# Splitting the layer-1 query weights ahead of the expert blocks, with six buffers for finished expert rows

## The reference, cut to what matters

```python
w, idx = jax.lax.top_k(p, TOPK)                       # 2 of 16 experts for each of 1024 tokens
gu = jnp.einsum('th,ehf->etf', x, gate_up_proj)
gate, up = jnp.split(gu, 2, axis=-1)
inter = jax.nn.silu(gate) * up
y = jnp.einsum('eti,eih->eth', inter, down_proj)
out = jnp.einsum('eth,te->th', y, combine)
...
q = (hidden_states @ Wq).reshape(N, t, H, DQ)         # layer 1; Wq is 256 x 2048
k = (hidden_states @ Wk).reshape(N, t, G, DQ)
v = (hidden_states @ Wv).reshape(N, t, G, DV)
```

## Time and profile before

| | us |
|---|---|
| median of 3 runs | 567.59 |
| lowest and highest | 564.04, 568.15 |
| profiled execution, its own time | 566.75 |
| span of that execution | 564.9 |

### The profile page before, as it was taken

The page is one execution under the profiler, slowest core; times in us unless marked ns, Lnnn a source line. Parts: engine busy times, 40 slices in busy tenths (PEclk is TensorE's granted clock), DMA queues, the critical chain, the costliest instruction groups (busy, mean ns, idle before and its releaser), DMA issues.

```text
span 564.9 us, 10664 instructions
## 1 busy us (share of the span) xinstructions
PE 508.0 (90%) x3547; PEld 438.8 (78%) x3570; DVE 394.8 (70%) x840; ACT 337.0 (60%) x755; POOL 308.7 (55%) x300
## 2 busy tenths in 40 slices
PE   8889999999996995699993798999999999999982
PEld 7568888888874884486772587999999899999882
DVE  2678888888872165749753688778866995578464
ACT  5546677777765244253340587768766866686552
POOL 4846777677763024639753168766544644466210
PEclk9999999999998997789996899999999999999996
DMA  8939999900000921243575000000000000000011
GB/s 279 391 113 372 305 323 316 313 13 0 0 0 1 368 116 56 82 128 106 160 253 209 23 0 2 1 1 1 2 2 0 1 1 2 2 1 2 1 38 39
DMA packets 17582, 56.80 MB, mean 101 GB/s; under 512 B 2580, under 2 KB 12314, under 8 KB 15738
## 3 DMA queue, kind: packets, MB, share of 16 engines
q1 hardware_dynamic: 14784, 49.81, 26.0%
q0 software_dynamic: 2752, 6.40, 3.2%
HBM read 49.19 MB, written 28.45 MB: 137 GB/s over the span
## 4 chain that ended last, share of the span: by engine, by line
PE 68%; DVE 10%; ACT 6%; issue 5%; DMA 5%; POOL 4%; SPq 1%; ACTq 0%; DVEq 0%; POOLq 0%
PE bank L435 10%; PE bank L437 8%; PE bank L436 8%; PE bank L483 5%; PE bank L525 4%; PE bank L544 3%; PE bank L906 3%; PE bank L527 2%; PE bank L668 2%; PE bank L653 2%; PE bank L655 2%; PE bank L654 2%; PE bank L555 2%; DMA wqk_raw<-in_wqk 2%; PE bank L923 2%
## 5 line engine op out<-in xcount | busy, mean ns | idle before, releaser
L999 ACT ACTIVATE probs<-bank,neg_max,q_scale 128x256 f32<-128x256 f32 (+1 forms) x128 | 63.7, 507 | 39.4 <-DVE neg_max L1565 39.4
L1775 POOL TENSOR_TENSOR probs<-probs,inv_sum 128x512 f32<-128x512 f32 x64 | 51.6, 827 | 44.0 <-DVE inv_sum L1573 44.0
L1808 POOL TENSOR_TENSOR exps<-exps,tables 128x256 f32<-128x256 f32 x32 | 25.2, 787 | 77.0 <-ACT exps L1092 77.0
L1795 POOL TENSOR_TENSOR swapped<-swapped,tables 128x512 f32<-128x512 f32 x32 | 42.9, 1339 | 24.0 <-ACT swapped L1030 23.8
L1092 ACT ACTIVATE exps<-bank 128x768 f32<-128x768 f32 x32 | 25.9, 810 | 42.2 <-PE bank L635 42.2
L1405 DVE TENSOR_TENSOR q_lo<-q_sum,q_hi 128x512 fp32r<-128x512 f32 x32 | 28.0, 877 | 28.4 <-ACT q_hi L1063 28.3
L1551 DVE TENSOR_TENSOR swapped<-bank,tables 32x512 f32<-32x512 f32 x64 | 44.4, 693 | 1.4
L1767 POOL TENSOR_TENSOR qT<-qT,swapped 128x512 f32<-128x512 f32 x32 | 40.8, 1274 | 7.1 <-DVE swapped L1551 7.1
L1911 POOL DMA_INDIRECT y_rows<-y_slot,dest x31 | 30.1, 972 | 23.7 <-DVE y_slot L1743 13.8
L435 PE MATMUL bank<-x,wq_hi 128*128 128x256 f32 x128 | 39.1, 306 | 2.7 <-DVE q_sum L1392 2.6
L525 PE MATMUL bank<-keysT,qT 128*128 128x256 f32 x128 | 38.3, 381 | 0.7 <-ACT wo_full L1214 0.7
(11 more groups left out here) (264 smaller groups left out, 1801.3 us busy)
## 6 DMA issues: line engine op xcount, KB each, us to landing
slots<-in_c_unused SPq DMA_DIRECT2D x20, 1036.0 KB, 36.9
gu_all<-in_gate_up SPq DMA_DIRECT2D x4, 1024.0 KB, 8.1
xg<-slots SPq DMA_DIRECT2D x31, 129.5 KB, 2.2
wvo_raw<-in_wvo SPq DMA_DIRECT2D x1, 2560.0 KB, 21.1
dn_all<-in_down SPq DMA_DIRECT2D x1, 2048.0 KB, 8.4
wq_full<-in_Wq SPq DMA_DIRECT2D x1, 2048.0 KB, 15.7
wo_raw<-in_Wo SPq DMA_DIRECT2D x1, 2048.0 KB, 10.7
yg<-y_rows SPq DMA_DIRECT2D x4, 512.0 KB, 5.2
```

Of the source, the lines that this page charges most:

```text
L999: ins = act.activation(probs[:, par, h, c0:c1], bank[:, 2 * par + h, c0:c1], ACT.Exp, bias=neg_max[:, par, i:i + 1], scale=q_scale[:, b, t ...
L1775: ins = pool.tensor_tensor(some, some, inv, ALU.mult)
L1795: pool.tensor_tensor(sw, sw, sin_rows(), ALU.mult).then_inc(at1["sin_done"], 1)
```

## The change

It has four parts.

1. **ACT**: the eight `wq_hi` copies stand in a row ahead of the first block's copy, behind the key and value copies, and none stands inside the blocks.
2. **POOL and DVE**: the key and value subtractions and the first four `wq_lo` chunks move from POOL to DVE, between the block table and `weights()`. POOL keeps the other four chunks, ahead of its first scatter of finished rows. None stands inside the blocks. A new semaphore `wq_lo` counts DVE's chunks.
3. **`y_slot`** has six buffers for four, so `copy_y(k)` waits for the landing of block k-6. KINDS (regions of filler rows, so that scatters in flight never write one address) grows from 6 to 8. `gated` and `act_tok` now lie in `swapped`, which is unused in this stage.
4. **SP** reads the block's address into a register before it waits for a free `xg` buffer, and no longer after.

```diff
-KINDS = 6
+KINDS = 8
+YS = 6
-        gated = sb("gated", [P, 2, FF], F32, blocks)
-        act_tok = sb("act_tok", [P, 2, FF], F32, blocks)
-        y_slot = sb("y_slot", [P, 4, D], F32, blocks)
+        y_slot = sb("y_slot", [P, YS, D], F32, blocks)
+    gated, act_tok = (swapped[:, i, 0:2 * FF].rearrange("p (i n) -> p i n", i=2) for i in range(2))
...
+        act.wait_ge(ld["wq1_in"], 16)
+        act.wait_ge(ln["y_done"], NT)
+        for i in range(PAIRS):
+            act.activation(chunk(wq_hi, i), chunk(wq_full, i), ACT.Copy).then_inc(kv["w_hi"], 1)
         copy_block(0)
         for k in range(STEPS):
             if k + 1 < STEPS:
                 copy_block(k + 1)
             silu(k)
-            if 2 <= k < 2 + PAIRS:
-                act.activation(chunk(wq_hi, k - 2), chunk(wq_full, k - 2), ACT.Copy).then_inc(kv["w_hi"], 1)
...
+        dve.wait_ge(kv["kv_hi"], 1)
+        dve.tensor_tensor(wk_lo[:], wk_raw, raw(wk_hi[:]), ALU.subtract).then_inc(kv["kv_lo"], 1)
+        dve.wait_ge(kv["kv_hi"], 2)
+        dve.tensor_tensor(wv_lo[:], wv_raw, raw(wv_hi[:]), ALU.subtract).then_inc(kv["kv_lo"], 1)
+        for i in range(PAIRS // 2):
+            dve.wait_ge(kv["w_hi"], i + 1)
+            dve.tensor_tensor(chunk(wq_lo, i), chunk(wq_full, i), raw(chunk(wq_hi, i)),
+                              ALU.subtract).then_inc(kv["wq_lo"], 1)
         weights()
...
-            if k >= 4:
-                dve.wait_ge(y_out[k % 4], 16 * (k // 4))
+            if k >= YS:
+                dve.wait_ge(y_out[k % YS], 16 * (k // YS))
...
-        pool.wait_ge(kv["kv_hi"], 1)
-        pool.tensor_tensor(wk_lo[:], wk_raw, raw(wk_hi[:]), ALU.subtract).then_inc(kv["kv_lo"], 1)
-        pool.wait_ge(kv["kv_hi"], 2)
-        pool.tensor_tensor(wv_lo[:], wv_raw, raw(wv_hi[:]), ALU.subtract).then_inc(kv["kv_lo"], 1)
+        for i in range(PAIRS // 2, PAIRS):
+            pool.wait_ge(kv["w_hi"], i + 1)
+            pool.tensor_tensor(chunk(wq_lo, i), chunk(wq_full, i), raw(chunk(wq_hi, i)),
+                               ALU.subtract).then_inc(kv["w_lo"], 1)
         for k in range(STEPS):
             pool.wait_ge(mo["dest_ready"], k + 1)
             pool.wait_ge(mo["y_copied"], k + 1)
             pool.indirect_dma_start(y_rows, ...)
-            if 3 <= k < 3 + PAIRS:
-                pool.wait_ge(kv["w_hi"], k - 2)
-                pool.tensor_tensor(chunk(wq_lo, k - 3), chunk(wq_full, k - 3), raw(chunk(wq_hi, k - 3)),
-                                   ALU.subtract).then_inc(kv["w_lo"], 1)
...
         for k in range(STEPS):
+            at_blocks = [sp.value_load(block_at[0:1, m:m + 1], ...) for m in ...]
             if k >= XG:
                 sp.wait_ge(mo["xgT_done"], k - XG + 1)
                 sp.wait_ge(mo["dest_ready"], k - XG + 1)
```

More of the change, by code:

```diff
@@ L288, in build @@
     xg_in = [sem(f"xg_in{j}") for j in range(XG)]
-    y_out = [sem(f"y_out{j}") for j in range(4)]
+    y_out = [sem(f"y_out{j}") for j in range(YS)]
     y_back = [sem(f"y_back{b}") for b in range(B)]
@@ L304, in build @@
               "xgT_done xgT_copied up_done silu_done act_ready actT_done actT_copied down_done y_copied dest_ready")
-    kv = sems("kv1", "kv_hi kv_lo w_hi w_lo k_done swap_done cos_done sin_done k_summed "
+    kv = sems("kv1", "kv_hi kv_lo w_hi wq_lo w_lo k_done swap_done cos_done sin_done k_summed "
               "k_hi k_lo v_done v_copied ones")
@@ L612, in pe_queries1 @@
             eng.wait_ge(kv["w_hi"], PAIRS)
-            eng.wait_ge(kv["w_lo"], PAIRS)
+            eng.wait_ge(kv["wq_lo"], PAIRS // 2)
+            eng.wait_ge(kv["w_lo"], PAIRS // 2)
         if m >= 2:
@@ L676, in pe_out1 @@
         if b == 0:
-            eng.wait_ge(kv["w_lo"], PAIRS + p + 1)
+            eng.wait_ge(kv["w_lo"], PAIRS // 2 + p + 1)
         elif p == 0:
@@ L1246, in _ @@
             silu(k)
-            if k == 2:
-                act.wait_ge(ld["wq1_in"], 16)
-                act.wait_ge(ln["y_done"], NT)
-            if 2 <= k < 2 + PAIRS:
-                act.activation(chunk(wq_hi, k - 2), chunk(wq_full, k - 2), ACT.Copy).then_inc(kv["w_hi"], 1)
         load_table(act, 2 * B + 8, ACT.Sqrt)
@@ L1740, in copy_y @@
             dve.wait_ge(mo["down_done"], k + 1)
-            if k >= 4:
-                dve.wait_ge(y_out[k % 4], 16 * (k // 4))
-            dve.tensor_copy(y_slot[:, k % 4, :], bank[:, down_bank(k), 0:D]).then_inc(mo["y_copied"], 1)
+            if k >= YS:
+                dve.wait_ge(y_out[k % YS], 16 * (k // YS))
+            dve.tensor_copy(y_slot[:, k % YS, :], bank[:, down_bank(k), 0:D]).then_inc(mo["y_copied"], 1)
         def find_rows(k):
@@ L1911, in _ @@
             pool.indirect_dma_start(y_rows, bass.IndirectOffsetOnAxis(ap=dest[:, k:k + 1], axis=0),
-                                    y_slot[:, k % 4, :], None).then_inc(y_out[k % 4], 16)
-            if 3 <= k < 3 + PAIRS:
-                pool.wait_ge(kv["w_hi"], k - 2)
-                pool.tensor_tensor(chunk(wq_lo, k - 3), chunk(wq_full, k - 3), raw(chunk(wq_hi, k - 3)),
-                                   ALU.subtract).then_inc(kv["w_lo"], 1)
+                                    y_slot[:, k % YS, :], None).then_inc(y_out[k % YS], 16)
         pool.memset(v_tok[:].rearrange("p b j g n -> p (b j g) n")[:, :, DV:DV + 1], 1.0).then_inc(kv["ones"], 1)
@@ L1943, in _ @@
         for i in range(REGIONS):
-            sp.dma_start(slots[i * REGION:(i + 1) * REGION, :], a["c_unused"][i % 4 if i < E else 4 + i % 2]).then_inc(ld["unused_in"], 16)
+            sp.dma_start(slots[i * REGION:(i + 1) * REGION, :], a["c_unused"][i % 6 if i < E else 6 + i % 2]).then_inc(ld["unused_in"], 16)
         sp.dma_start(wk_raw, a["Wk1"]).then_inc(ld["wkv1_in"], 16)
@@ L1954, in _ @@
         for k in range(STEPS):
+            at_blocks = [sp.value_load(block_at[0:1, m:m + 1], min_val=0, max_val=UNITS + NB - 1)
+                         for m in range(PER_STEP * k, PER_STEP * k + PER_STEP)]
             if k >= XG:
@@ L1957, in _ @@
                 sp.wait_ge(mo["dest_ready"], k - XG + 1)
-            for i in range(PER_STEP):
-                m = PER_STEP * k + i
-                at_block = sp.value_load(block_at[0:1, m:m + 1], min_val=0, max_val=UNITS + NB - 1)
+            for i, at_block in enumerate(at_blocks):
                 sp.dma_start(xg[ROWS * i:ROWS * i + ROWS, k % XG, :],
@@ L1963, in _ @@
         sp.dma_start(wo1_raw[:], a["Wo1"].rearrange("(h p) n -> p h n", p=P)).then_inc(ld["wo1_in"], 16)
-        for j in range(4):
-            sp.wait_ge(y_out[j], 16 * len(range(j, STEPS, 4)))
+        for j in range(YS):
+            sp.wait_ge(y_out[j], 16 * len(range(j, STEPS, YS)))
         for b in range(B):
```

## The result

| | before | after |
|---|---|---|
| median, us (4 runs each, same chip) | 567.38 | 560.98 |
| lowest and highest | 564.04, 568.15 | 559.11, 561.86 |
| profiled execution, its own time | 566.75 | 561.69 |
| its span | 564.9 | 559.9 |

The ratio of the times is 0.9882 with a 95% interval from 0.9835 to 0.9929: faster by 1.2%. The interval excludes no change, but it has a gain of 1% inside, so "over 1%" is likely and not certain; the change run again (e4) has 0.9892 (0.9854 to 0.993). The forecast of 562.3 lay 1.3 us above the median, and the range holds it. The median thus fell on the side to which the prediction gave the smaller chance (0.36 for over 1%, 0.61 for within 1%).

A forecast was written before the change was run, and what follows sets the result against it. The prediction took PE as the bound, held up in seven block rounds by POOL's subtraction holding DVE's `find_rows`. It summed 5.0 + 0.7 - 0.4 = 5.3 us, for a median of 562.3 us, range 560.3 to 566.0.

The forecast's parts named there:

- The loop: Expert blocks: the seven rounds with subtractions go at PE's 1.64 us each, 5.0 us less, bounds 4.8 to 5.3.
- It is therefore the subtraction that holds DVE's instruction: Blocks from 257 to 273.5 us: POOL's subtraction, not its scatter, stretches `find_rows` (L1747) from 0.21 to 1.81 us.
- part 1: The prediction's first term: no subtraction inside the blocks, so slow rounds reach PE's pace, 5.0 us less.
- The start: Ahead of the blocks: DVE's and POOL's subtractions run end to end, costing PE 0 to 0.7 us, taken as 0.4.
- The tail: End of the blocks: six buffers spare `copy_y` its wait for landings, 0.7 us less, bounds 0 to 0.9.
- ACT, SP, filler rows: ACT's moved copies, SP's earlier address reads and more filler regions: each forecast to be worth nothing.
- The start did not slip: Rival ahead of the blocks: DVE waits longer and PE starts at its lower clock, 565.3 us; chance 0.12.
- The buffers bought 0.98: Rival at the end: landings under the 2 MB load are the limit, six buffers gain nothing, 563.0 us; chance 0.12.
- The subtractions left the blocks: Rival: DVE wins every turn, POOL's four run to 243 us and hold the first `find_rows`, 563.1 us; chance 0.05.
- The last scatters into `slots` were not held: Rival ahead of the blocks: DVE's subtractions hold these scatters, all behind comes 7.1 us later, 569.0 us; chance 0.05.
- the 236.4: Sign in the changed profile: a first `xg` load later than 236.4 us would mean the scatters were held.
- Everything behind the load back ... stays as it is.: After the blocks: all behind the load back at 303.59 us shifts earlier and keeps its length.

The follow-up runs named there:

- e11: The kernel before with `find_rows` rewritten to read one tensor with two per-partition scalars, POOL's subtractions left in the blocks: 569.55 us, ratio 1.0005.
- e1: The change with four `y_slot` buffers and six filler regions, SP's address read behind its wait again: 560.54 us, ratio to before 0.9908.
- e3: The kernel before with the eight `wq_lo` subtractions still inside the blocks, but on DVE instead of POOL: 559.56 us, ratio 0.9894.
- e10: The kernel before with six `y_slot` buffers and the `wq_lo` subtractions on DVE inside the blocks: 559.5 us, ratio 0.9861.
- e7: The change with all key, value and `wq_lo` subtractions on POOL ahead of the blocks, DVE's six removed: 566.5 us, ratio 0.9975.
- e5: The change with 65 dummy matmuls on PE ahead of its wait for the load back: 558.58 us, ratio 0.9829.
- e8: The change with SP's address reads behind the wait for a free buffer again, as before: 559.58 us, ratio 0.9839.
- e9: The change with 45 dummy matmuls on PE ahead of its wait for the load back: 560.01 us, ratio 0.9845.
- e2: The kernel before with only six `y_slot` buffers and eight filler regions, subtractions still inside the blocks: 563.62 us, ratio 0.9958.
- e12: The kernel before with six buffers, `wq_lo` subtractions on DVE inside the blocks and 45 dummy matmuls: 559.43 us, ratio 0.9849.
- e6: The change with POOL's four `wq_lo` chunks also done by DVE, so DVE has all eight: 559.36 us, ratio 0.9832.

## Why the prediction was right, and where its reasons were not

**The loop (5.0 forecast, 5.33 measured).** The mechanism's place and its size were right: rounds of 2.46 became rounds of 1.63, with PE busy throughout. What failed is the sentence "It is therefore the subtraction that holds DVE's instruction", taken as the cause of the lost time. The hold is real (e11 and the change both remove it), but e11 removes the hold alone and gains nothing. The limit is POOL's own round: scatter 0.99, 0.17, subtraction 1.28, with 0.03 of gaps 2.47 us, against PE's 1.63. The hold, or four full buffers, then passes that pace on to PE: with the held `find_rows` PE's rounds are slow from block 11 on, and without it, through the buffers, from block 16 on. Whether the hold would cost nothing with more buffers is not shown (see e11). POOL was on record as busy for 15.03 of 16.51 us in the earlier trace rows, which is 0.91 of the time, and I had read the small rest as the sign that DVE held it. The remedy is the one of part 1 for either cause, and so the number came out right, in part by luck; the 5.33 lies just above the upper bound of 5.3. e1, e3 and e10 show that it is enough that the subtractions leave POOL's rounds.

**The start (-0.4 forecast, +0.96 measured).** DVE was free sooner than forecast, for two reasons. DVE's and POOL's subtractions did not cost their full sum end to end: from 234.0 to 241.0 us eight chunks took 7.0 us, four pairs of about 1.7, where 0.68 + 1.28 makes 1.96. And the idle 0.7 us before a held instruction did not come back (in e7 it did: L1692 stands from 233.47, POOL's first subtraction starts at 234.16). `p_top` was done at 242.26, 10.4 us behind the table's last row, where the forecast had 11.8 to 12.5. Even so the price to PE is 0.2 to 0.6 us where the clock is full: 15.26 to 15.30 from the table to block 4 in the change, e1, e4, e5, e8 and e9, against 15.08, 14.81 and 14.65 in e2, e10 and e12, which have before's program there. The 0.4 was thus a fair size. What the term lacks is the clock, worth 1.1 to 1.6 us: before's execution had the lower level for most of 242 to 244 us, and the change's had 1.00:

```profile
242.00:244.00 2.00, 1.58 (x9) 1.06 (x8) 1.26 (x7) 0.73 (x3) 0.00 (x0) 1.00 0.29 70
```

Whether the change brings that is open. Of six kernels with before's program there, three have the lower level (before, e3, e11, 15.94 to 16.22) and three don't (e2, e10, e12). None of the six with the change's program has it. But e6, with all subtractions of that place on DVE, has it again (15.75), so free blocks do not by themselves keep it away.

The Trainium skill, page "SBUF — State Buffer", section "Summary: rules for kernel authors", says that of two such instructions, one on DVE and one on POOL, the one that comes second blocks fully until the first has finished. The four pairs agree in the main: each chunk is on record for its own time and most of the other's. But a pair took about 1.7 us, less than the 1.96 of both alone. e7 does not agree: there a second-comer stood through ten, 15.14 us, so the rule gives no bound on the wait. The rule of the Trainium skill in the section "Who interferes with whom" of that page, that a DVE instruction with at most one SBUF input, outside its 2-port modes, does not contend with POOL, agrees with e11 (0.27 us, 31 times of 31).

**The tail (0.7 forecast, 0.98 measured).** The mechanism was right, and it is the buffers: 6.56 in e1 and 6.47 in e3 with four, 5.43 or 5.44 in every kernel with six. It came out just above the upper bound of 0.9.

**ACT, SP, filler rows (nothing).** Right: e8 equals the change, and PE is busy without a gap from block 4 to block 29, whatever ACT does.

**The rivals.** The start did not slip (0.2 to 0.6 us). The buffers bought 0.98. The subtractions left the blocks. The last scatters into `slots` were not held: the one that ran beside DVE's 1024 columns took 1.17 us in place of 0.98, and the first `xg` load was issued 5.31 us behind the table, before the change 5.45. By the clock of the view that load came at 237.01, later than the 236.4 that the prediction named as a sign of held scatters, but only because the table itself came 0.71 us later. That was the one case that would have made the kernel slower.

**"Everything behind the load back ... stays as it is."** This failed by 1.5 us in three executions of the change's program out of three (259.09, 259.06, 259.20). The clock is at 0.50 from 296.4 us until 313.2:

```profile
292.00:296.20 4.20, 0.27 (x2) 0.00 (x0) 0.56 (x2) 0.00 (x0) 2.99 (x4) 1.00 0.29 115
296.40:300.40 4.00, 0.00 (x0) 0.00 (x0) 0.00 (x0) 0.00 (x0) 0.00 (x0) 0.50 0.57 158
...
306.40:313.20 6.80, 5.34 (x25) 5.17 (x25) 2.71 (x8) 3.47 (x6) 0.00 (x0) 0.50 0.01 2
313.60:317.60 4.00, 4.00 (x30) 3.69 (x28) 2.69 (x4) 3.59 (x6) 2.19 (x2) 1.00 0.00 0
```

PE has nothing to do from 292.3 until the dummies of layer 1 at 300.9, and the clock falls in that pause; before, the same pause lay from 298.8 to 307.5, and the clock, low from 301.7, was up again at 311.9, ahead of the first product at 314.20. In the change the products come first, at 308.06. Of the other kernels e1, e6, e7 and e11 have the 4.37 us of before, and e2, e3, e5, e9, e10 and e12 have 5.7 to 7.1. e1 is the change but for buffers, so it is not the split ahead as such. Behind the first value product the kernels fall into three groups, and again the lower level tells them apart. e2, e3, e5 and e10 have full clock there until 540 us and take 243.5 to 243.8 us. The change, e4, e8, e9 and e12 have one stretch of 3.4 us at about 340 us and take 245.0 to 245.1. Before, e1, e6, e7 and e11 have one or two times that right behind the products and take 246.2 to 246.9. A window of each group, in that order (e5, the change, before):

```profile
337.00:345.00 8.00, 5.90 (x50) 5.71 (x50) 6.84 (x12) 7.14 (x13) 6.84 (x7) 1.00 0.01 3
...
340.70:344.10 3.40, 3.27 (x16) 3.31 (x17) 2.38 (x4) 2.62 (x5) 3.40 (x3) 0.50 0.00 0
...
322.20:325.60 3.40, 2.94 (x13) 2.65 (x13) 2.76 (x4) 2.46 (x5) 1.28 (x1) 0.50 0.01 2
```

So the lost 1.5 us go with the low stretches: 16.0 us of them between the read and 500 us in the change, 8.0 before. What decides where they fall I can't say, and so it stays open whether this loss belongs to the change: neither kind of dummies settled it.

**The sum.** The terms were too small by 0.33, 1.36 (the clock's part of the start is 1.1 or more of it) and 0.28, together 2.0 us, and 2.2 us were lost outside, 0.71 of it spread: 5.07 of span against 5.3. The profiled executions thus agree with the forecast (561.69 against 561.45) partly by luck: two errors cancel. The median came out lower than forecast because the changed kernel's profiled execution lay 0.7 above its median, where the forecast, going by the runs before, had added 0.84 to it.

## What to carry to other kernels

When two engines are slow together, add up each one's own work in a round before blaming a hold between them: POOL's 0.99 + 1.28 us already exceeded PE's 1.63, and taking the hold away (e11) moved the wait to the buffers and gained nothing. More buffers alone gained nothing in the loop either (e2); both together were not tried. Work stops costing when it leaves the engine that is over the bound, and another engine with room in the same round is as good as a place ahead of the loop (e3, e10). Where a DVE instruction that reads two SBUF tensors stands next to a row of POOL's subtractions, allow for its waiting out the whole row (e7), and put nothing behind it that PE needs.

## What the runs showed of the hardware

- The same two kinds of instruction take turns or don't. 512-column subtractions on DVE and POOL alternated in the change, 7.0 us for four of each. A 16-column one on DVE waited out ten on POOL (15.14 us), as L1693 had waited out two. What gives DVE its turn is open.
- An indirect scatter of POOL is slowed a little by DVE reading two SBUF tensors: the last one into `slots` takes 1.17 us beside a 1024-column subtraction in all seven kernels that have it there, and 0.97 in the seven that don't.
- The same matmuls of layer 1 took 6.73 us where the granted clock was 0.50 for the first 5.3 of them (the change) and 4.37 where it was 1.00 throughout (before), and more dummies ahead of them did not reliably change that: e9 had full clock in a pause and the low one in the products.
- One kernel's executions within a batch differ by 2 to 7 us. In three profiled ones with the change's blocks (the change, e4, e8) the loop is equal to 0.01 us, and the differences lie outside it: the block table came at 231.70 and 229.57 us in two executions of the same program, which had 6.8 and 3.4 us at the lower clock level ahead of it.
